# Finding each node's first edge by searching the sorted destinations, in place of a histogram of destinations and a stage that lists the edges

## The reference

```python
# layer 0 (row = src, col = dst; loops added)
h = relu(layernorm(x))
deg = segment_sum(concat(w, 1), row)
dinv = where(deg > 0, rsqrt(deg), 0)
out = segment_sum(dinv[row] * w * dinv[col] * (h @ kernel)[col], row)
x = x + relu(out + bias)
# layer 1
h = relu(layernorm(x))
agg = segment_sum(concat([h[src], E]) @ W_fwd + b_fwd, dst) \
    + segment_sum(concat([h[dst], E]) @ W_back + b_back, src)
cnt = segment_sum(1, dst) + segment_sum(1, src)
agg = agg / (cnt + 1e-7)
x = x + gamma * layernorm(leaky_relu(agg) + h) + beta
```

## Time and profile before

| | us |
|---|---|
| median of 3 runs | 4618.35 (4617.26 to 4620.77) |
| the profiled execution, its own time | 4623.39 |
| span of the profiled execution | 4621.6 |
| PE busy | 3497.9 (76%) |
| DVE busy | 3319.0 (72%) |
| POOL busy | 2905.8 (63%) |
| ACT busy | 1864.9 (40%) |

### The profile page before, as it was taken

The page is one execution under the profiler, slowest core; times in us unless marked ns, Lnnn a source line. Parts: engine busy times, 40 slices in busy tenths (PEclk is TensorE's granted clock), DMA queues, the critical chain, the costliest instruction groups (busy, mean ns, idle before and its releaser), DMA issues. The chain is left out here.

```text
span 4621.6 us, 103887 instructions
## 1 busy us (share of the span) xinstructions
PE 3497.9 (76%) x32143; PEld 2940.4 (64%) x32143; DVE 3319.0 (72%) x8239; ACT 1864.9 (40%) x4498; POOL 2905.8 (63%) x1711
## 2 busy tenths in 40 slices
PE   3555307988988888889991359989889889899955
PEld 2545306777777777777770347767767767777645
DVE  8999728878888888888881477766666666666427
ACT  1011005545555555555550424444444444444513
POOL 0000076888888888888883068877888777788300
PEclk8777658999999999999995659999999999999977
DMA  9990116777777777777778655555555545555761
GB/s 167 304 132 0 43 22 134 137 134 145 139 134 139 137 135 138 136 135 136 138 139 129 122 103 83 81 81 77 81 81 79 80 75 79 78 82 82 90 126 28
DMA packets 678459, 503.84 MB, mean 109 GB/s; under 512 B 305948, under 2 KB 591012, under 8 KB 676296
## 3 DMA queue, kind: packets, MB, share of 16 engines
q0 software_dynamic: 256832, 174.75, 34.5%
q1 hardware_dynamic: 421092, 322.34, 29.1%
HBM read 283.21 MB, written 240.09 MB: 113 GB/s over the span
## 5 line engine op out<-in xcount | busy, mean ns | idle before, releaser
L707 POOL DMA_INDIRECT gcn_sums<-fl_sums,fl_to_i x864 | 1470.1, 1702 | 307.4 <-DMA gcn_sums<-fl_sums,fl_to_i 151.7
L1535 POOL DMA_INDIRECT gcn_sums<-shared,ds_to_i x752 | 1303.3, 1733 | 533.4 <-ACT shared L1787 319.9
L1742 PE MATMUL bank<-ds_counts,ds_parts 128*128 128x256 bf16 x3675 | 605.9, 278 | 0.0
L1811 ACT COPY ds_turned<-bank 128x1024 bf16<-128x1024 bf16 (+1 forms) x325 | 313.1, 963 | 602.1 <-PE bank L1727 503.7
L931 ACT COPY fl_sums<-bank 128x256 f32<-128x256 f32 x864 | 324.0, 375 | 558.0 <-PE bank L859 416.0
L1775 ACT CAST ds_counts<-bank 128x392 bf16<-128x392 f32 x800 | 382.7, 490 | 225.7 <-PE bank L1686 204.5
L744 DVE SCALAR_TENSOR_TENSOR fl_same<-fl_key_b,fl_pat,from_me 128x128 f32<-128x128 bf16 x864 | 374.1, 445 | 132.0 <-PE bank L859 110.2
L1762 PE MATMUL bank<-ds_turned,ds_now 128*128 128x512 bf16 (+1 forms) x1950 | 463.4, 375 | 0.0
L372 PE MATMUL bank<-places,row_hot 128*128 128x200 bf16 x1616 | 268.4, 293 | 254.3 <-DVE places L325 254.3
L1671 DVE TENSOR_TENSOR src_sums<-src_sums,bank 128x512 f32<-128x512 f32 (+1 forms) x325 | 213.3, 656 | 259.3 <-PE bank L1762 254.5
L1704 PE MATMUL bank<-shared 128*128 128x128 f32 x1504 | 307.7, 309 | 116.7 <-DVE attr_sums L1588 88.1
(11 more groups left out here) (236 smaller groups left out, 7786.0 us busy)
## 6 DMA issues: line engine op xcount, KB each, us to landing
fl_attrs<-in_edge_attr SPq DMA_DIRECT2D x108, 512.0 KB
shared<-in_edge_attr SPq DMA_DIRECT2D x186, 256.0 KB
fl_rel_b<-dst_offset SPq DMA_DIRECT2D x108, 256.0 KB
fl_key_b<-src_key SPq DMA_DIRECT2D x108, 256.0 KB
gcn_sums<-zeros SPq DMA_DIRECT2D x40, 640.0 KB
shared<-src_key SPq DMA_DIRECT2D x94, 256.0 KB
gcn_sums<-fl_sums,fl_to_i POOLq DMA_INDIRECT x864
near<-src_float SPq DMA_DIRECT2D x1, 12892.0 KB
```

Source lines behind the costliest of these rows:

```text
L707: nc.gpsimd.indirect_dma_start(out=d.tab_gcn[j % K], out_offset=bass.IndirectOffsetOnAxis(ap=to_i[:, (GPI * kk + gi) % 4, j:j + 1], axis=0 ...
L1535: nc.gpsimd.indirect_dma_start(out=d.tab_gcn[j % K].rearrange("n (two f) -> (n two) f", two=2), out_offset=bass.IndirectOffsetOnAxis(ap=to ...
L1742: ins = nc.tensor.matmul(row_bank[:, 0:2 * P], parts[:, tile, s, :], counts[:, h, tile, :, :].rearrange("p b q -> p (b q)"), start=(tile = ...
```

## The change

`dst_lists` is gone as a block. The histogram counts sources alone. The first edge of each node is found by a search in three steps, each beside the histogram: DVE compares each node with 101 destinations (one in 2,048 edges), POOL gathers for each tile a row of 128 samples (one in 16 edges), DVE compares and counts, POOL gathers a row of 16 keys, DVE compares and counts again, and that is `start`. Then POOL gathers the rows of `near` and `near_w` as before, still beside the histogram. DVE's part of each step stands at the end of one of the now six sections of the chunk loop. The counts of destinations come from the differences of `start`. Tiles that were free by then are used again (`near` lies on the edges, `hi` on `rec`, the compared rows on `attr_sums`).

```diff
-        row_hot = sb("row_hot", [P, 2, 2, WJ, P], BF16)
+        row_hot = sb("row_hot", [P, 2, WJ, P], BF16)
...
-        SECTIONS = ((1, AT, "offsets"), (AT, THEN, "deviations"), (THEN, NG // 4, None))
+        SECTIONS = ((1, 14, "search_rows"), (14, 20, "offsets"), (20, 27, "search_edges"), (27, 33, "deviations"), (33, 42, "places"), (42, NG // 4, None))
...
+            sp.wait_ge(runs_ready, 5)
+            sp.dma_start(lines(d.dst_f), dst_run).then_inc(dst_stored, 16)
+            for a, t in ((d.samples, samples[:]), (d.dst_key, key16[:, 1, :]), (d.src_f, src_run), (d.w_f, w_run),
+                         (d.src_key, key16[:, 0, :]), (d.src_i, src_i), (d.dst_i, dst_i)):
+                sp.dma_start(lines(a), t).then_inc(runs_stored, 16)
+            sp.wait_ge(dst_stored, 16)
+            sp.dma_start(heads[:], d.dst_f.rearrange("(o k e) -> o k e", o=1, e=COARSE * FINE)[:, :, 0:2]).then_inc(heads_in, 16)
+            sp.dma_start(next_first[0:P - 1, :], d.dst_f.rearrange("(p c) -> p c", c=EC)[1:P, 0:2]).then_inc(heads_in, 16)
...
+            pool.wait_ge(row_ready, 1)
+            pool.sem_inc(turns, 1)
+            for t in range(TILES):
+                fetch(rows2[:, t, :], d.samples.rearrange("(k c) -> k c", c=COARSE), row_i[:, 0, :], t, rows2_in)
+            pool.wait_ge(row_ready, 2)
...
+                fetch(rows3[:, t, :], d.dst_key.rearrange("(k c) -> k c", c=FINE), row_i[:, 1, :], t, rows3_in)
+            pool.wait_ge(row_ready, 3)
+            pool.wait_ge(near_stored, 32)
...
+                fetch(near[:, t, :], d.near, row_i[:, 2, :], t, near_in)
+            pool.wait_ge(rec_stored, 16)
...
+                fetch(near_w[:, t - T0, :], d.near_w, row_i[:, 2, :], t, near_w_in)
+            nc.gpsimd.memset(d.attr_sums[:], 0.0).then_inc(ident_ready, 1)
...
+            link(nc.vector.tensor_tensor(row_f[:, 1:EC], dst_run[:, 1:EC], dst_run[:, 0:EC - 1], ALU.subtract))
+            dve.wait_ge(heads_in, 32)
+            link(nc.vector.tensor_tensor(row_f[:, 0:1], next_first[:, 0:1], dst_run[:, EC - 1:EC], ALU.subtract))
+            link(nc.vector.tensor_reduce(bad[:, 0:1], row_f[:], AX_X, ALU.min))
...
+            def search_heads():
+                dve.wait_ge(heads_spread, 1)
+                dve.wait_ge(runs_stored, 16 * 7)
+                link(nc.vector.tensor_tensor(less1, head_bank[:, 0:HEADS].unsqueeze(1).to_broadcast([P, TILES, HEADS]), per_node(node, HEADS), ALU.is_lt))
+                link(nc.vector.tensor_reduce(found[:], less1, AX_X, ALU.add))
...
+            def search_rows():
+                dve.wait_ge(rows2_in, 16 * TILES)
+                link(nc.vector.tensor_tensor(less2, rows2, per_node(node_key, COARSE), ALU.is_lt))
+                link(nc.vector.tensor_reduce(found[:], less2, AX_X, ALU.add))
...
+            def search_edges():
+                dve.wait_ge(rows3_in, 16 * TILES)
+                link(nc.vector.tensor_tensor(less3[:], rows3[:], per_node(node_key, FINE), ALU.is_lt))
...
+            def places():
...
+                dve.wait_ge(near_in, 16 * TILES)
...
             def one_hots(i, h):
...
-                for m, cols in enumerate((col_w[:, h, :, 3, :], col_hot[:, h, :, :])):
-                    nc.vector.tensor_tensor(in_twos(cols), counted(NT), pair(col_of[:, m, :, :], NT), ALU.is_equal).then_inc(step, 1)
-                    nc.vector.tensor_tensor(in_twos(row_hot[:, h, m, :, :]), counted(P), pair(row_of[:, m, :, :], P), ALU.is_equal)
+                nc.vector.tensor_tensor(in_twos(col_w[:, h, :, 3, :]), counted(NT), pair(col_of, NT), ALU.is_equal).then_inc(step, 1)
+                nc.vector.tensor_tensor(in_twos(row_hot[:, h, :, :]), counted(P), pair(row_of, P), ALU.is_equal)
...
-            nc.vector.tensor_tensor(x[:], x[:], d.dinv[:].unsqueeze(2).to_broadcast([NP, NT, F]), ALU.mult).then_inc(g_ready, 1)
+            for r in range(2):
+                part = x[:, r * HT:(r + 1) * HT, :]
+                nc.vector.tensor_tensor(part, part, d.dinv[:, r * HT:(r + 1) * HT].unsqueeze(2).to_broadcast([NP, HT, F]), ALU.mult).then_inc(g_ready, 1)
+            split_weights()
...
 def first_layer(nc, d):
...
+            nc.gpsimd.memset(d.gcn_t[:], 0.0).then_inc(gcn_zeroed, 1)
```

More of the change, by code:

```diff
@@ L185, in _ @@
                 sp.dma_start(t, groups(a)).then_inc(rec_in, 16)
-            for near, of in ((d.near, d.src_f), (d.near_w, d.w_f)):
-                sp.dma_start(near, bass.AP(of.tensor, 0, [[STEP, NEAR], [1, SLOTS]])).then_inc(stored, 16)
+            for near_table, of in ((d.near, d.src_f), (d.near_w, d.w_f)):
+                sp.dma_start(near_table, bass.AP(of.tensor, 0, [[STEP, NEAR], [1, SLOTS]])).then_inc(near_stored, 16)
             sp.wait_ge(zeroed, 1)
@@ L328, in _ @@
             one_hots(0, 0)
+            search_heads()
             one_hots(0, 1)
+            hooks = {"search_rows": search_rows, "offsets": offsets, "search_edges": search_edges, "deviations": deviations, "places": places}
             for begin, end, then in SECTIONS:
@@ L334, in _ @@
                         one_hots(i, h)
-                if then == "offsets":
-                    offsets()
-                if then == "deviations":
-                    deviations()
+                if then:
+                    hooks[then]()
             dve.wait_ge(hot_used, NG // 2 - 2)
@@ L370, in chunks @@
                 for j in range(WJ):
-                    ends = dict(start=first and j == 0, stop=last and j == WJ - 1)
-                    nc.tensor.matmul(hist[:, 0:4 * NT], row_hot[:, h, 0, j, :], col_w[:, h, j, :, :].rearrange("p s n -> p (s n)"), **ends)
-                    done_with = nc.tensor.matmul(hist_dst[:, 0:NT], row_hot[:, h, 1, j, :], col_hot[:, h, j, :], **ends)
+                    done_with = nc.tensor.matmul(hist[:, 0:4 * NT], row_hot[:, h, j, :], col_w[:, h, j, :, :].rearrange("p s n -> p (s n)"),
+                                                 start=first and j == 0, stop=last and j == WJ - 1)
                 done_with.then_inc(hist_ready if last else hot_used, 1)
+            pe.wait_ge(heads_in, 32)
+            pe.wait_ge(iota_ready, 4)
+            nc.tensor.matmul(head_bank[:, 0:HEADS], d.ones[0:1, :], heads[:, :, 0], start=True, stop=True).then_inc(heads_spread, 1)
             chunks(0, 0, True, False)
             chunks(0, 1, False, False)
+            hooks = {"offsets": offsets, "search_edges": search_edges, "places": places}
             for begin, end, then in SECTIONS:
@@ L510, in _ @@
[L510 to L523 removed]
+            dve.wait_ge(run_in, 16)
@@ L525, in _ @@
+            one_hots(0, 0)
+            one_hots(1, 1)
+            with dve.Fori(1, EC // 2) as i:
+                for h in range(2):
+                    dve.wait_ge(hot_used, 2 * i + h - 1)
+                    one_hots(2 * i + h, h)
+            dve.wait_ge(hot_used, EC)
+            link(nc.vector.tensor_copy(d.cnt_dst[:], hist[0:NP, 0:NT]))
+            nc.vector.tensor_tensor(d.cnt[:], d.cnt_src[:], d.cnt_dst[:], ALU.add)
         @block.tensor
         def _(pe):
-            pe.wait_ge(cnt_ready, 1)
```

434 lines of the change are left out of this document (242 added, 192 removed).

## The result

The changed kernel takes **4404.06 us** (median of 4 runs: 4403.20, 4403.89, 4404.23 and 4448.90) against 4617.81 for the kernel before on the same chip (4 runs, 4613.51 to 4620.77). The ratio is 0.9565, with a 95% interval of 0.9513 to 0.9617; the 4448.90 makes it that wide. The forecast was 4397, in a range of 4372 to 4440. A later repeat of the same kernel gave 4405.82 and a ratio of 0.9544 (0.9526 to 0.9563).

A forecast was written before the change was run, and what follows sets the result against it. DVE was taken to set the pace. DVE's 452.2 us plus a 30.1 us tail start the first layer at 482.3, not 704.22; gain 220.8 from 4623.4 gives 4402.6, less 5.0 for the median: 4397 us, range 4372 to 4440.

The forecast's parts named there:

- What goes: Destination one-hots leave each chunk, 4.70 to 3.08 us over 101 chunks; the list stage's 139.2 us go whole.
- The start: DVE waits for `heads_in` until 47.5 us; first chunk at 66.9, everything behind it 22.3 us later.
- What DVE gets: Added search work on DVE: `search_heads` 11.7 us, `search_rows` 15.1, `search_edges` 6.0, `places` 21.4.
- PE's turn: After `places`, PE turns 50 tiles in 10.85 us; DVE fills two buffers meanwhile, leaving a 7.4 us wait.
- The gathers: POOL's gathers beside chunks: two per chunk, 1.54 us each, 82.3 us a set, all covered and costed at nothing.
- The warning that the prediction takes from the summary: Trainium skill's warning of descriptor generation starved under VectorE, cited as speaking against the gathers step.
- The 70 us of cover: Chunks behind `places` cover the 26 gathers of `near_w` and POOL's clearing, which need 45 to 60 us.
- The end: DVE's sum 452.2 us, then a 30.1 us tail; first layer begins at 482.3; `gcn_t` memset costs 1.1 us.
- The last step, from 4402.6 to 4397: 5.0 us taken off because the kernel before's median stood that much below its profiled execution.
- PE's clock: PE in the chunk loop at the slower clock level: a chunk takes it 2.7 us, under DVE's 3.08.
- the rival in which PE becomes the bound: Unpipelined 200-column matmuls at 0.34 us make a chunk 5.4 us, 234 us more, about 4631; chance 0.02.

The follow-up runs named there:

- run 2: Kernel before, with the destinations' one-hots and matmuls left out of its chunks and their counts set to the constant 33: 4511.78 us.
- Run 1: Changed kernel with the check that destinations are sorted, and its wait for two loads, moved behind chunk 0: 4375.63 us, ratio 0.947.
- run 3: Changed kernel with the first search section ended after 14 chunks instead of 26, a shorter cover for the samples' gathers: 4416.35 us.
- run 4: Changed kernel with `gcn_t` cleared only after DVE's first copy in the first layer: 4399.09 us, ratio 0.9517.
- run 7: Changed kernel with PE's second, 50-column matmul of each pair put back into an unused bank, DVE's chunk as changed: 4575.04 us.
- run 5: Changed kernel with the order check behind chunk 1, sections cut at 15, 20, 28, 33, 42 and `gcn_t` cleared late: 4368.23 us, ratio 0.946.
- run 11: Changed kernel with the order check behind chunk 1, late `gcn_t` clearing, PE's loop unrolled to four chunks, cuts 15, 21, 27, 33, 43: 4376.93 us.
- run 12: Changed kernel with only the section cuts moved to 15, 21, 27, 33, 43, PE's loop as it was: 4407.32 us, ratio 0.9545.
- run 10: Changed kernel with PE's loop over chunks unrolled to four chunks, sections cut at 15, 21, 27, 33, 43: 4386.19 us, ratio 0.948.
- run 9: Changed kernel with PE's matmul pairs put back and all searches and gathers moved behind the last chunk: 4596.75 us.
- run 8: Changed kernel with destinations' one-hots put back on DVE (from sources' numbers, one more wait per chunk) and matmul pairs on PE: 4598.44 us.

## Why the prediction was right

Point by point, by its own steps.

- **What goes.** Right. The chunk is 3.08 us in the trace, and run 2 takes 165.3 us out by that part alone, of the 224.4 by which the setup and the list stage are shorter together. The rest is the list stage, less the searches and the later start.
- **The start.** Predicted: heads at 47.5, first chunk at 66.9; measured 46.59 and 65.95. Run 1 shows that the wait is avoidable, worth 20 us: it was priced well, and taken as given.
- **What DVE gets.** `search_heads` 11.2 (predicted 11.7), `search_rows` 179.5 - 165.2 = 14.4 (15.1), `search_edges` 281.8 - 276.7 = 5.1 (6.0), `places` 397.5 - 376.2 = 21.3 (21.4). Prices per element, read from rows of other types, held within 10%; only the many small instructions came cheaper than their round number.
- **PE's turn.** 4.03 us against 7.4. The turning took 8.2 us, not the 10.85 of the old list stage, and the chunk behind it 1.9 until DVE went on, not 2.7:

```profile
397.66 1.11 PE L563 MATMUL bank<-ident,edges_i 128*128 128x128 f32 x4 [19.75 <-DVE rec L486]
...
405.70 0.33 PE L563 MATMUL bank<-ident,rec 128*128 128x128 f32 x1
405.88 2.92 PE L585 MATMUL bank<-col_w,row_hot 128*128 128x200 bf16 x32
```

- **The gathers.** Right at 1.54 us, and right in the mechanism as far as the runs reach. The samples' set lasts from 80.3 to 165.1 us, 84.8 where the prediction had 82.3, hence the wait of 1.65. In run 3 the 32.48 us of wait are what the missing six iterations of cover make by that price, and the price falls to 1.24 once DVE stands still. By the Trainium skill, "SBUF — State Buffer", section "Who interferes with whom", POOL and DVE share a pair of ports as an exclusive lock, held for a whole instruction; the trace agrees: a gather ends 0.8 us after the end of a DVE instruction (97.11 after 96.29), as it did at 593.10, and two fit in each chunk. The warning that the prediction takes from the summary of that page of the Trainium skill is given there for VectorE's 2x and 4x modes alone, which the prediction leaves out; no row here tells the modes apart. Beside the longer instructions of `places` six gathers of `near_w` take 2.26 to 3.39 us, this one beside two of 3.48:

```profile
377.42 3.10 POOL L287 DMA_INDIRECT rec<-near_w,row_i  x1 [0.30 <-issue]
```

  The 70 us of cover hide that.
- **The end.** 452.48 + 1.53 = 454.0 for DVE's last chunk instruction, against 452.2, and a tail of 26.1 us, not 30.1. PE's last matmuls keep DVE waiting 1.64 us, not 3.33, and from the end of the multiply to the first layer it is 480.1 - 464.9 = 15.2 us where the prediction, with half a multiply beside the store, had 17.7. The clearing of `gcn_t` costs DVE 5.40 us rather than 1.1, but run 4 took that away and the first scatter came no sooner behind SP's first issue: DVE has to wait for the first records in any case.
- **What the sum lacked.** 6.1 us of waits for PE near 240 us. They and the 1.65 of the samples nearly cancel against 6.5 us of terms that came cheaper, which is luck; with the tail 4.0 shorter, the first layer begins at 480.1, predicted 482.3.
- **The last step, from 4402.6 to 4397.** The profiled execution was predicted at 4402.6 and took 4403.89: the setup 2 us under, the layers 4.9 us longer than before where 1.1 was predicted, which no run explains. The 5.0 us taken off for the median held for the kernel before; here the profiled execution lies at the median, and most of the 7 us between 4397 and 4404.06 is this step.
- **PE's clock.** The prediction took PE at the lower level throughout. The granted clock was 0.97 between 84 and 165 us (0.78 in the kernel before, in the same stretch), and a chunk took 1.55 us, not 2.7. That made the rival in which PE becomes the bound even less likely on its own terms. But it came near in another way: with the pairs left on PE (run 7) PE does hold DVE up, 169 us for the worse, by a mechanism that the prediction has nowhere. The part of the change that looked like a mere saving on an idle engine, one matmul in place of two, is what the rest stands on.

**The waits near 240 us: what is shown and what is open.** PE there, in the changed kernel:

```profile
226.92 0.19 PE L551 MATMUL bank<-ones,wide 128*1 128x1 f32 x2 [7.70 <-DVE wide L453]
230.25 2.85 PE L585 MATMUL bank<-col_w,row_hot 128*128 128x200 bf16 x16 [3.14 <-issue]
233.32 2.74 PE L585 MATMUL bank<-col_w,row_hot 128*128 128x200 bf16 x16 [0.23 <-issue]
236.67 1.55 PE L585 MATMUL bank<-col_w,row_hot 128*128 128x200 bf16 x16 [0.61 <-issue]
242.52 2.77 PE L585 MATMUL bank<-col_w,row_hot 128*128 128x200 bf16 x16 [4.30 <-DVE col_w L507]
```

PE comes out of a pause at the lower level (2.85 us for 16 matmuls, against 1.55), hardly under DVE's 3.08. DVE should go on at 236.6 with the buffer that PE left at 236.06, but goes on at 239.29. Its wait is for the chunk before last, and yet it lasts past the end of the last one.

Run 4, with the same code in the setup and no such waits, has nearly the same two chunks behind the pause:

```profile
229.40 2.85 PE L585 MATMUL bank<-col_w,row_hot 128*128 128x200 bf16 x16 [3.14 <-DVE col_w L507]
232.48 2.42 PE L585 MATMUL bank<-col_w,row_hot 128*128 128x200 bf16 x16 [0.23 <-DVE col_w L507]
```

Shown: the waits come behind `offsets`, beside the gathers of the keys, in six traces (the changed kernel, its repeat, runs 5, 11 and 12, and far longer in run 7), and not in four (runs 1, 3, 4 and 10), nor in run 9, where no gathers lie there. The same six traces, and run 8, mark some of PE's idle time ahead of the wide matmuls as "issue", always beside gathers (5.5 us in the changed kernel, 12.9 in its repeat, 18.1 in run 8, 87.9 in run 7); the four without the waits have none, nor have the kernel before and runs 2 and 9, where no gathers lie beside chunks.

Not shown: whether PE runs its matmuls later than its records say, or signals them late, or gets its instructions late, as the gaps in run 7 suggest; and what about the gathers does it. The lower level alone does not decide it (run 4), nor the setup's own code (4), nor the length of PE's loop (10, 11), nor the cuts (12), nor the DMA traffic (9), nor the loading of code. It may need PE to be close behind DVE: at 5.09 us a chunk (run 8) PE has its 18.1 us of "issue", and DVE waits for none of them. That is a guess from one run.

## What to carry to other kernels

Work moved beside a loop is free only while the loop's own engines have room: here the gathers cost DVE about 8 us of waits beside 16 matmuls per chunk (6.1 near 240 us and 1.65 for the samples), and 180 beside 32, with DVE's instructions unchanged in both. Price each moved step by its own rows, give every wait its cover in us, and then ask of the engines that seem idle what slack they keep. And put a check that nothing depends on for a long time behind the first piece of work, not ahead of it: that alone took 20 us off, more than all finer edits together.

## What was not expected of the hardware

- Gathers by POOL can go with stalls of PE, an engine that shares no data with them: matmuls 0.7 us or more apart with no semaphore to wait for, 180.4 us of waits in run 7, and two waits of 0.66 in run 9 without them. Each is one execution.
- POOL's MEMSET of 6,400 elements (5.43 us) holds a CAST of 128 elements on DVE for 5.40 us, which took 0.22 at 65.69.
- PE's granted clock did not follow the number of its matmuls. Between 84 and 165 us it was 0.78 with 32 matmuls per 4.70 us (the kernel before) and 0.79 with 32 per 5.09 (run 8), 0.97 with 16 per 3.08 (the changed kernel), and 1.00 per 3.08 without gathers, with 16 (run 2) as with 32 (run 9). Where PE stalled (run 7) it was 0.65.
- The layers, with the same code but for the clearing of `gcn_t`, took from 3910 to 3927 us over these kernels (3970.8 in run 2): as much as the finer edits to the setup. Those had to be judged by the time at which the first layer begins.
